# Low parts of the down weights by a negated high part and an accumulating transfer

## What is computed

```
gate = silu(xg @ rg[e]);  up = xg @ ru[e]          # 8 experts, 97 tokens each, 1024 -> 4096
eout = (gate * up) @ rd[e]                          # 4096 -> 1024
shared = (silu(x @ sg) * (x @ su)) @ sd             # all 625 tokens, 1024 -> 8192 -> 1024
out = x + shared + routed(eout, weights of the two experts of each token)
```

## Time and profile before

| | us |
|---|---|
| median of 3 runs | 3019.35 |
| lowest, highest | 3015.39, 3023.61 |
| profiled execution | 3022.32 |
| its span | 3020.7 |

### The profile page before, as it was taken

The page is one execution under the profiler, slowest core; times in us unless marked ns, Lnnn a source line. Parts: engine busy times, 40 slices in busy tenths (PEclk is TensorE's granted clock), DMA queues, the critical chain, the costliest instruction groups (busy, mean ns, idle before and its releaser), DMA issues.

```text
span 3020.7 us, 44215 instructions
## 1 busy us (share of the span) xinstructions
PE 2957.7 (98%) x16902; PEld 2508.6 (83%) x16902; DVE 1919.4 (64%) x2562; ACT 1261.4 (42%) x1592; POOL 63.4 (2%) x81
## 2 busy tenths in 40 slices
PE   8999999799999999999999999999999999999997
PEld 8997999688888888888888888888888888888876
DVE  8745244666666666666666666666666666666675
ACT  7622221444444444444444444444444444444451
POOL 0100000100000000000000000000000000000001
PEclk9999999899999999999999999999999999999999
DMA  3110110566666666666666666666666666666674
GB/s 107 36 57 29 57 57 12 176 203 209 209 219 209 209 209 221 209 209 209 221 209 209 209 221 209 209 209 221 209 209 209 220 210 209 209 214 209 209 244 158
DMA packets 257984, 549.23 MB, mean 182 GB/s; under 512 B 8612, under 2 KB 74404, under 8 KB 257637
## 3 DMA queue, kind: packets, MB, share of 16 engines
q1 hardware_dynamic: 253826, 532.16, 52.1%
q0 software_dynamic: 3936, 14.06, 1.5%
HBM read 537.49 MB, written 8.70 MB: 181 GB/s over the span
## 4 chain that ended last, share of the span: by engine, by line
PE 92%; DVE 3%; DMA 3%; ACT 1%; issue 1%; SPq 0%; DVEq 0%; ACTq 0%
PE ps L1531 25%; PE ps L1529 25%; PE ps L1530 25%; PE ps L1289 3%; PE ps L1345 3%; PE ps L1346 3%; PE ps L1344 3%; PE ps L1404 2%; DVE c_lo L1148 1%; PE ps L1329 1%; DMA raw<-in_L_ffn_rd 1%; PE ps L1565 1%; DMA raw<-in_L_ffn_su 1%; PE ps L1442 1%; PE ps L1441 1%; PE ps L1440 1%
## 5 line engine op out<-in xcount | busy, mean ns | idle before, releaser
L1148 DVE TENSOR_TENSOR c_lo<-raw,c_hi 128x1024 fp32r<-128x1024 f32 x960 | 1126.5, 1221 | 318.3 <-ACT c_hi L667 317.1
L667 ACT CAST c_hi<-raw 128x1024 fp32r<-128x1024 f32 x960 | 953.1, 1048 | 462.3 <-DMA raw<-in_L_ffn_rg 131.3
L1529 PE MATMUL ps<-yT_hi,c_hi 128*128 128x314 f32 (+1 forms) x2048 | 629.1, 307 | 1.1 <-issue 1.1
L1530 PE MATMUL ps<-yT_lo,c_hi 128*128 128x314 f32 (+1 forms) x2048 | 629.0, 307 | 0.4 <-issue 0.4
L1531 PE MATMUL ps<-yT_hi,c_lo 128*128 128x314 f32 (+1 forms) x2048 | 628.5, 307 | 0.3 <-issue 0.3
L1531 PE MATMUL ps<-c_hi,xgT_lo 128*97 128x512 f32 x1024 | 403.4, 394 | 0.0
L1529 PE MATMUL ps<-c_hi,xgT_hi 128*97 128x512 f32 x1024 | 402.2, 393 | 1.0 <-DVE xgT_lo L1176 1.0
L1530 PE MATMUL ps<-c_lo,xgT_hi 128*97 128x512 f32 x1024 | 401.3, 392 | 0.0
L1529 PEld LDWEIGHTS ps<-yT_hi,c_hi 128*128 128x128 f32 x2048 | 386.7, 189 | 3.7 <-issue 1.1
L1530 PEld LDWEIGHTS ps<-yT_lo,c_hi 128*128 128x128 f32 x2048 | 387.1, 189 | 1.8 <-issue 0.5
L1531 PEld LDWEIGHTS ps<-yT_hi,c_lo 128*128 128x128 f32 x2048 | 386.7, 189 | 0.5 <-issue 0.5
(11 more groups left out here) (227 smaller groups left out, 3376.4 us busy)
## 6 DMA issues: line engine op xcount, KB each, us to landing
raw<-in_L_ffn_rg SPq DMA_DIRECT2D x128, 1024.0 KB, 5.5
raw<-in_L_ffn_ru SPq DMA_DIRECT2D x128, 1024.0 KB, 6.6
raw<-in_L_ffn_rd SPq DMA_DIRECT2D x128, 1024.0 KB, 5.9
raw<-in_L_ffn_sg SPq DMA_DIRECT2D x32, 1024.0 KB, 6.2
raw<-in_L_ffn_su SPq DMA_DIRECT2D x32, 1024.0 KB, 5.9
raw<-in_L_ffn_sd SPq DMA_DIRECT2D x32, 1024.0 KB, 6.1
wl<-in_L_mix_w_qkv SPq DMA_DIRECT2D x6, 2048.0 KB, 7.8
wl<-in_L_gnn_W SPq DMA_DIRECT2D x2, 2048.0 KB, 29.3
```

The source lines that it names most:

```text
L667: nc.scalar.copy(order.view(c_hi[u % RING], u), part(raw[r % RAW])).then_inc(sem("hi_done"), 1)
L1148: V.tensor_tensor(order.view(c_lo[u % RING], u), part(raw[r % RAW]), order.view(c_hi[u % RING], u).bitcast(F32), ALU.subtract).then_inc(se ...
L1529: MM(out_, l_hi, r_hi, start=first, stop=False)
L1530: MM(out_, l_hi, r_lo, start=False, stop=False)
```

## The change

The eight down units of a step are left out of DVE's `lo`. Instead ACT, after `c_hi`, reads the same part of `raw` once more and writes the rounded value negated into `c_lo` (activation `Copy` with scale -1.0) and counts `neg_done`. GpSimd waits for that count and issues a transfer that reads the 128 x 1024 weights from DRAM again and adds them onto `c_lo` in place. Each of the eight has a semaphore of its own (`down_lo0` to `down_lo7`), for which TensorE waits in `split`. SP gives a raw buffer of down units back on `neg_done` instead of `lo_done`; `lo_done` counts 22 units a step now. GpSimd's loop over the experts is written out (unrolled), with the 32 additions of an expert behind its `turn_over` and `gather`.

```
+DOWN = 8
+SPLIT = U - DOWN
+    def down(self, u):
+        return self.rd <= u < self.rd + DOWN
+    def lo_index(self, u):
+        return u if u < self.rd else u - DOWN
...
@@ block.sync
+        def given_back(e, q, step, order, u):
+            if order.down(u):
+                sp.wait_ge(sem("neg_done"), count(e, q, DOWN, step * DOWN + u - order.rd + 1))
+            else:
+                sp.wait_ge(sem("lo_done"), count(e, q, SPLIT, step * SPLIT + order.lo_index(u) + 1))
...
-                    sp.wait_ge(sem("lo_done"), count(e, q, U, U + order.last_unit[b - RAW] + 1))
+                    given_back(e, q, 1, order, order.last_unit[b - RAW])
                 else:
-                    sp.wait_ge(sem("lo_done"), count(e, q, U, STEP.last_unit[b - RAW + BLK] + 1))
+                    given_back(e, q, 0, STEP, STEP.last_unit[b - RAW + BLK])
...
@@ block.gpsimd
+        def add_raw(e, q, order=STEP):
+            for r in range(DOWN):
+                pool.wait_ge(sem("neg_done"), count(e, q, DOWN, DOWN + r + 1))
+                pool.dma_start(c_lo[(order.rd + r) % RING][:], rd_v[e, q][:, r, :],
+                               accum_op=ALU.add).then_inc(sem(f"down_lo{r}"), 16)
-        with pool.Fori(0, E - 1) as e:
+        for e in range(E - 1):
             turn_over(e)
...
             gather()
+            for q in range(Q):
+                add_raw(e, q)
         turn_over(E - 1)
+        for q in range(Q):
+            add_raw(E - 1, q, LAST if q == Q - 1 else STEP)
...
@@ block.scalar, hi(u)
                 nc.scalar.copy(order.view(c_hi[u % RING], u), part(raw[r % RAW])).then_inc(sem("hi_done"), 1)
+                if order.down(u):
+                    nc.scalar.activation(c_lo[u % RING][:], part(raw[r % RAW]), ACT.Copy,
+                                         scale=-1.0).then_inc(sem("neg_done"), 1)
...
@@ block.vector
-        dve.sem_inc(sem("lo_done"), U)
+        dve.sem_inc(sem("lo_done"), SPLIT)
+        dve.sem_inc(sem("neg_done"), DOWN)
...  lo(u)
+                if order.down(u):
+                    return
...
@@ block.tensor, split(u)
-                pe.wait_ge(sem("lo_done"), count(e, q, U, U + u + 1))
+                if order.down(u):
+                    pe.wait_ge(sem(f"down_lo{u - order.rd}"), count(e, q, 16, 16))
+                else:
+                    pe.wait_ge(sem("lo_done"), count(e, q, SPLIT, SPLIT + order.lo_index(u) + 1))
```

## The result

| | us |
|---|---|
| changed kernel, median of 4 runs | 3317.17 (3316.15 to 3334.52) |
| kernel before, beside it | 3019.67 (3015.39 to 3023.61) |
| ratio | 1.1002, 95% interval 1.0972 to 1.1032 |
| profiled execution after, its span | 3334.52, 3332.8 |

It is 297.5 us slower by the medians, a ratio of 1.0985. The ratio in the table takes in all executions, for the changed kernel two more of 3326.36 and 3321.27 us. 3377 us was predicted, with 3110 to 3560 as the likeliest case's own range and 3010 to 3850 as the whole. The traces compare profiled executions, and there the difference is 312 us.

What follows compares the result with a forecast made beforehand. TensorE was taken as the bound, with 8.8 us idle. Late additions, 31 steps x 11 = 341 us, and 17 for the last step on 3022.3 gave 3380, less 3.0: 3377 us, range 3010 to 3850.

Steps and rivals of the forecast that it cites:

- likeliest case: Additions at the two-source price stall TensorE 3 to 17 us a step: 3110 to 3560 us, chance 0.42.
- VectorE's relief: VectorE loses 9.8 us a step, costed at 0; as a rival, 8.8 us gained in all, 3011 us, chance 0.03.
- An addition costs two sources, 2.65 us: A 512 KB addition on the DMA engines fetches 1024 KB, so takes 2.65 us, like a raw block.
- The bounds at 1.32 and 5.3: Limits in us for one addition: below, a plain 512 KB transfer; above, twice 2.65 if adding halves the engines' pace.
- the slow adder: Rival: an addition takes 3.3 us or more; 3726 us at 4.0, some 4200 at 5.3; chance 0.27.
- A full window: From 1528.5 to 1555.7 us, 39.8 us of transfers for 27.2, though a step needs only 61 of 75.8.
- Half to two thirds of the engines for the additions: Share beside raw blocks before the down matmuls: last addition 16.4 or 6.0 us late, 11 taken, paid every step.
- my own sum: End of the last addition: start at 1528.5, eight additions' 21.2 us stretched by their share, plus 1.2 overhead; needed by 1555.7.
- The last step, 17 us: In the last step, five raw blocks and eight additions end late for unit 23: 19 or 16 us, 17 taken.
- ScalarE and GpSimd at 0: ScalarE's 8 extra us a step fit its 10.83 us wait, GpSimd's 4.7 its idle time: both cost 0.
- The signs: Profile after: some five `c_lo` waits a step, PE slices at 8 tenths, landing 8 us or more, no new `r_h` wait.
- The shared engines: GpSimd's transfers run on the same 16 DMA engines and interleave with the rest; a private path would make the change free.

Runs made afterwards that it cites:

- e9: Changed kernel with the additions on units 4 to 11 instead of 22 to 29, all eight of an expert's first step ahead of `turn_over`: 3072.48 us, 1.0179.
- e2: Changed kernel with the 256 transfers as plain copies that overwrite `c_lo`, without adding: 3026.40 us, ratio 1.0034 to the kernel before.
- e10: Changed kernel with each of the 256 additions covering 512 of the 1024 columns: 3027.90 us, ratio 1.0033 to the kernel before.
- e3: Changed kernel with additions for only the first four down units (22 to 25), the last four through VectorE as before: 3106.40 us, ratio 1.0314.
- e6: e3 with `routed_add` after low parts 0 to 3 and low parts 28, 29 later among VectorE's shared additions: 3025.82 us, ratio 1.0028.
- e7: Kernel before, with bursts of copies and additions after its last store, some beside raw blocks: eight copies 13.3 us, eight additions 23.3 us.
- e4: Changed kernel with `routed_add` on VectorE after the low parts of units 0 to 3 instead of 0 to 9: 3189.18 us, ratio 1.0569.
- e1: Changed kernel without the 256 additions; ScalarE's extra passes, GpSimd's waits and the unrolled loop stay: 3028.69 us, ratio 1.0044.

## Why the prediction was right, and where not

*TensorE bounds, VectorE's relief gives nothing.* Right: VectorE's share fell from 64% to 49% and no run with it is faster than before.

*An addition costs two sources, 2.65 us.* The price is right: 2.51 to 2.55 us alone, 2.67 by the queue's share. The bounds at 1.32 and 5.3 are both out, and with them the slow adder. That the reason is the second read is not shown: no view counts what an addition reads from its destination, and an adder at half the pace of a copy would look the same. The rule of the Trainium skill that I gave beside it (Collectives: The Full Stack, The bandwidth ceiling: the fold count and why AG ≠ RS ≠ AR) is stated there for the reduce step of a ring between cores. The ratio here agrees with it: 407 against 209 GB/s is 1.95.

*A full window, not a lack of average capacity.* Right, by e9 (all additions elsewhere, 75.7 us a step) and by e2 and e10 (half the engine time, no cost). Half as many cost 89 us in e3, and 6 us with another order on VectorE (e6).

*Half to two thirds of the engines for the additions.* The step that failed in part. The share goes by rows, not by bytes (e7): beside 4 KB rows the additions get two thirds, beside the 2 and 1 KB rows of most raw blocks 78 and 91%. With 0.8 my own sum gives 1528.5 + 21.2 / 0.8 + 1.2 = 1556.2, half a us late instead of 6 to 16. So the additions were hardly late (12.2 us to landing, 62.4 us of waits in all), and the blocks behind them were very late. I had all 11 us a step in front of the down matmuls, and held that the engines catch up in the shared matmuls without a further price. Measured from 620 to 3200 us, 30 steps, are 56.4 us of waits for additions, 53.5 for low parts of the next step's first units, 84.1 for `routed_add`, which I had not thought of, and 20.7 of others: 1.9, 1.8, 2.8 and 0.7 a step, and some 3 in TensorE's slower work. So the total of 10.0 came near the 11 with one fifth of it where I had put all. That is luck in good part, as e4 shows: one place in VectorE's order was worth 128 us of the 297, with the same transfers.

*The last step, 17 us.* From the copy of `eout` that stands twelve steps before the end (2296.64 us after, 2102.27 before) to the end of the span it is 1036.2 us after and 918.4 before: 117.8 us more, and less 11 steps of 10.0 that leaves 8.

*ScalarE and GpSimd at 0.* Off by 12 us for the three edits together (e1), 0.4% and so just beyond what can be told from no change. ScalarE's pass takes 1.055 us as assumed, and the 10.83 us of cover were there. But `hT_hi` moved inside them, and VectorE's shared additions behind `turned_lo(0)` with it. I had checked that TensorE does not need `hT_lo` and not what else is queued behind it.

*The signs.* The additions land after 12.2 us, over the 8 I named; the engines stay full from 1640 to 1670 us; and a wait names the DMA. But there are 57 such waits in 32 steps and not five a step, the slices of PE fall to 9 tenths more than to 8, and `r_h` has a new wait of 9.0 us in the last step.

*The shared engines.* The Trainium skill's rule (DMA: Bandwidth & Descriptors, Issuing engines are not separate DMA queues) agrees with e7. Eight additions and three blocks in long rows take 30.6 us from the first issue to the last landing. Eight additions alone take 23.3, and three blocks at 407 GB/s would hold the engines for 7.7 us, as an estimate: together 31.0.

Open: how much of the 3 us a step is the clock's own cost. In the step shown the clock fell behind the longest stall and not behind the two shorter ones; in e4, without that stall, it was 0.986 over the whole (0.992 before). No run changed the clock alone.

## What to carry to other kernels

Here an accumulating transfer cost the DMA engines what a copy of twice its bytes costs (2.51 against 1.29 us for 512 KB in rows of 4 KB); sum this over the stretch in which it must be done and not over the step. When a stream is late, look at what each engine has queued behind the instruction that uses it: here moving finished-result additions ahead of the next low parts gave back 128 us in one kernel and 81 in another, more than the transfers' own waits. And an engine with spare time, as VectorE here, is no reason to put its work on a resource that is full.

## What the runs showed of the hardware

- Additions write 209 GB/s, copies 407, with all 16 engines busy; a source in SBUF makes them no faster (200).
- Two queues on the same engines share them as if they took turns by row: beside eight additions in 4 KB rows, 3 MB landed within 18.5 us in 4 KB rows, 27.4 in 2 KB rows and 32.3 in 1 KB rows, and all together took 30.6, 31.4 and 33.3 us.
- GpSimd takes 0.85 us to issue an addition of 128 rows, of 4 KB or of 2 KB (e10), 1.17 us for one of 256 rows (e9), and 0.53 for a copy of 128 rows in e2. In e7's burst of eight additions it takes up to 3.3 us for one.
- After TensorE's wait of 3.45 us that ends at 1689.93 the granted clock was 0.69 and 0.88 in the stretches from 1688 and 1692 us; after its waits between 1668 and 1672.37 it stayed at 1.00 until then.
